# Moving the gates, the carry factor and the squares of a state-space kernel between engines, with a new order per stage

## The chip, the cores and the metric

The kernel runs on one core of a Trainium2 chip. The metric is the device time of one execution in microseconds (us), the median of several runs. Everything is float32.

## What is computed

Input x has 8 sequences of 1024 steps and 256 channels. The first half is a selective state-space layer (512 inner channels, 16 states each), the second a mixture of 8 experts, top 2, with capacity 768; both have a residual and a layer norm. The part that matters here:

```python
xn = x * rsqrt(mean(x * x) + 1e-6) * norm_w
x_branch, gate = split(xn @ W_in.T)
xc = causal_conv4(x_branch) + conv_b
xc = xc * sigmoid(xc)
dt = soft_clamp(softplus(xc @ W_dt.T + b_dt), 0.001, 0.1, 0.5)      # a tanh
Bp, Cp = xc @ W_B.T, xc @ W_C.T
dA = exp(soft_clamp(dt[..., None] * A, -8, 8, 0.5))                 # tanh, then exp
# for each step t:
h = h * dA_t + dt_t * B_t * x_t                                     # h: 8 x 512 x 16
if t % 10 == 0: h = h * min(20 / (norm(h) + 1e-8), 1)               # one norm per sequence
y_t = h . C_t + D * x_t
out = x + scale * (y * gate * sigmoid(gate)) @ W_out.T
```

## The kernel before

`ssm_phase` walks 52 stages of 20 time steps for all 8 sequences. A stage is cut into four quarters q (10 steps for 4 sequences), a quarter into four sequences u; `s` = 0 to 15 numbers these slots. Each engine has its own program, one loop over i (stage) and s (slot) with `if s == ... and ok(i + k)` blocks, and runs it strictly in that order; semaphores `s_...` tie the programs together. So the place of a block in an engine's list decides what waits behind it. Work for stage i+2 or i+3 is prepared while stage i is scanned.

- **VectorE** has per slot `mult` (L579, dt x B, 640 elements) and `scan` (L610, 704 elements, the recurrence over 10 steps); every two slots `carry` (L596) puts the start state, already multiplied by the norm factor (CAR), into PSUM. It adds `norm_sum` (L617), `z_out` (L631), `dt_x` (L566), the gate products XC (L647, slot 6) and SG (L705, slot 15), VV (L697), and the copy of the router logits LGS (L714).
- **ScalarE** computes the decays in DA: 64 tangents per stage (L514, spread over the slots by the list `DUE`) and four large exponentials (`exp_a`, L377). It also makes the squares SQ for the norm (L398) and of x (L408), copies out of PSUM (L417, L423, L458 to L467, L475), the tangents of the two gates, since x sigmoid(x) = x/2 (1 + tanh(x/2)) (L430, L499), and the dt chain of exponentials, logarithm and tangent (L451, L481, L489). Two activation tables are loaded per stage, at L481 and L489.
- **GpSimd** multiplies H by C (L775), makes the norm factor FC by a power of -0.5 (L755) and CAR (L760), and does DT (L737), XN (L743), the layer norm of VV, and DX.
- **TensorE** sums H C over the 16 states by identity matmuls (`y_sum`, L820; each fp32 matmul shows as two records, 34 records per quarter with L816), the norms (L862), the sum of squares of x (L873), the projections of branches and gates (`project`, L826), the convolution as diagonal matmuls (L836) with its bias (L832), dt (L845), B and C (L902), the output projection (L921), transposes (L911), and router logits (L930). All but the y sums share two PSUM banks, PA and PZ, in turn; `wait_free` waits for the reader of the use before.

The order of the shared banks before, and where a stage's gate is released:

```python
        users_pa = [
            (3, s_ms, lambda j: j + 1),
            (2, s_xb, lambda j: j + 1),
            (2, s_xc, lambda j: j + 1),
            (2, s_ex, lambda j: 4 * j + 2),
            (-2, s_x2t, lambda j: j + 1),
            (1, s_sg, lambda j: j + 1),
            (-2, s_lgs, lambda j: j + 1),
        ]
```

`moe_phase` with the experts follows and is not touched.

## Time and profile before

| | |
|---|---|
| median of 3 runs | 2773.73 us (2773.64 to 2775.39) |
| span of the profiled execution, first to last instruction | 2772.7 us |
| PE, DVE, ACT, POOL busy | 94%, 86%, 81%, 77% of the span |
| mean granted TensorE clock | 0.975 of full speed |
| scan phase | to about 2315 us of the span |

PE is TensorE, DVE VectorE, ACT ScalarE, POOL GpSimd. The profiled execution has no time of its own besides its span; the runs' median is 1.0 us above it. A duration in the timeline holds the end of an instruction, during which the next already runs, so the step from start to start is shorter than the duration. The granted clock is a share of full speed: 1.00 is 2.4 GHz, 0.50 is 1.2 GHz.

### The profile page before, as it was taken

To read this page: it belongs to the slowest core of one execution; us is meant where nothing else is said; L and a number is where in the kernel's file an instruction comes from. 1 tells how busy PE (TensorE), PEld (TensorE's weight loads), DVE (VectorE), ACT (ScalarE), POOL (GpSimd) and SP (SyncE) were. 2 spreads that over 40 slices of the span, in tenths; PEclk is the share of its full clock that TensorE was granted. 3 is DMA by queue.
4 is the path that set the end of the run, shared out by engine and by line. 5 is a ranking of instruction groups with operands and counts; after the bars stand their busy time and mean duration, and the time that the engine had idled before them with its cause. 6 is when DMAs were issued, how large, how long until landed. Compare 5 with 4: busy or idle time off the path is not lost. (4 is left out here: it accounts for less than half of the span.)

```text
span 2772.7 us, 50775 instructions
## 1 busy us (share of the span) xinstructions
PE 2593.0 (94%) x16812; PEld 2388.8 (86%) x16812; DVE 2382.4 (86%) x3391; ACT 2245.1 (81%) x5074; POOL 2134.4 (77%) x2237
## 2 busy tenths in 40 slices
PE   5899999999999999999999999999999986899992
PEld 4899999999999999999999999999999975677762
DVE  2999999999999999999999999999999997221124
ACT  5999999999999999999999999999999962111113
POOL 0789888898898988989889889898898883434314
PEclk9899999999999999999999999999999987999996
DMA  1222222222222222222222222222222222234227
GB/s 61 70 78 78 79 80 78 78 78 81 77 78 75 80 79 78 78 78 82 78 78 78 81 78 78 76 78 80 78 78 78 75 78 93 48 93 105 61 48 254
DMA packets 145746, 225.65 MB, mean 81 GB/s; under 512 B 37836, under 2 KB 84684, under 8 KB 144332
## 3 DMA queue, kind: packets, MB, share of 16 engines
q1 hardware_dynamic: 123044, 188.95, 22.4%
q0 software_dynamic: 9216, 12.59, 2.6%
q10 hardware_dynamic: 13224, 20.86, 2.2%
q8 instruction: 134, 2.20, 0.3%
q14 instruction: 128, 1.05, 0.1%
HBM read 189.27 MB, written 33.05 MB: 80 GB/s over the span
## 5 line engine op out<-in xcount | busy, mean ns | idle before, releaser
L775 POOL TENSOR_TENSOR H<-H,CB 128x640 f32<-128x640 f32 (+1 forms) x832 | 1216.2, 1476 | 157.1 <-DVE H L610 154.9
L610 DVE TENSOR_TENSOR_SCAN H<-DA,PM 128x704 f32<-128x704 f32 (+1 forms) x832 | 1309.4, 1594 | 0.0
L514 ACT ACTIVATE DA<-DT,SM 128x160 f32<-128x160 f32 (+1 forms) x3328 | 1106.8, 421 | 1.6 <-POOL DT L737 0.3
L820 PE MATMUL YB<-H,ID 128*128 128x160 f32 (+1 forms) x6656 | 1043.9, 309 | 0.2 <-POOL H L775 0.2
L820 PEld LDWEIGHTS YB<-H,ID 128*128 128x128 f32 x6656 | 982.3, 191 | 16.4 <-issue 11.2
L579 DVE TENSOR_TENSOR PM<-PM,BB 128x640 f32<-128x640 f32 (+1 forms) x832 | 673.1, 809 | 0.0
L377 ACT ACTIVATE DA<-DA 128x2560 f32<-128x2560 f32 (+1 forms) x206 | 477.7, 2319 | 1.7
L755 POOL TENSOR_TENSOR FC<-SN,HALF 128x4 f32<-128x4 f32 x206 | 232.8, 1130 | 40.8 <-DVE SN L617 36.8
L826 PE MATMUL PAZ<-XN,RB 128*128 128x160 f32 x1664 | 254.7, 307 | 0.1
L836 PEld LDWEIGHTS PAZ<-XB,CD 128*128 128x128 f32 x1664 | 237.5, 188 | 16.8
L845 PE MATMUL PAZ<-XC,RB 128*128 128x160 f32 x1664 | 244.4, 300 | 3.3 <-DVE XC L647 3.3
L1285 POOL DMA_INDIRECT YA<-YS,IG x48 | 75.1, 1566 | 219.8 <-ACT YS L1116 208.2
L836 PE MATMUL PAZ<-XB,CD 128*128 128x160 f32 x1664 | 243.1, 297 | 0.0
L826 PEld LDWEIGHTS PAZ<-XN,RB 128*128 128x128 f32 x1664 | 237.9, 195 | 0.7 <-ACT CS L467 0.3
L845 PEld LDWEIGHTS PAZ<-XC,RB 128*128 128x128 f32 x1664 | 231.1, 190 | 6.4 <-DVE XC L647 4.0
L921 PE MATMUL PAZ<-WO,Z 128*80 128x256 f32 x832 | 189.1, 380 | 0.0
L862 PE MATMUL YB<-SQ,MEAN 128*128 128x128 f32 x824 | 131.3, 282 | 43.0 <-ACT SQ L398 43.0
L760 POOL TENSOR_TENSOR CAR<-H,FC 128x256 f32<-128x256 f32 x206 | 155.4, 754 | 17.3
L921 PEld LDWEIGHTS PAZ<-WO,Z 128*80 128x80 f32 x832 | 125.3, 151 | 49.4 <-issue 0.7
L1359 PE MATMUL PE<-W,HT 128*128 128x256 f32 x768 | 167.2, 379 | 0.8 <-issue 0.8
L1348 PE MATMUL PE<-XTE,W 128*128 128x384 f32 x512 | 167.3, 488 | 0.0
L1359 PEld LDWEIGHTS PE<-W,HT 128*128 128x128 f32 x768 | 145.3, 190 | 20.8 <-issue 1.3
(157 smaller groups left out, 2779.7 us busy)
## 6 DMA issues: line engine op xcount, KB each, us to landing
BB<-Bd SPq DMA_DIRECT2D x208, 320.0 KB, 3.4
CB<-Cd SPq DMA_DIRECT2D x208, 320.0 KB, 3.2
W<-in_w ACTq DMA_DIRECT2D x16, 1024.0 KB, 7.9
XT<-in_xT SPq DMA_DIRECT2D x52, 160.0 KB, 2.2
XR<-in_xp SPq DMA_DIRECT2D x208, 40.0 KB
X2d<-VV SPq DMA_DIRECT2D x208, 40.0 KB
YA<-VV SPq DMA_DIRECT2D x208, 40.0 KB
HI<-YA SPq DMA_DIRECT2D x6, 1024.0 KB, 9.9
```

The source lines that it names most:

```text
L377: eng.activation(v, v, ACT.Exp, scale=16.0).then_inc(s_da, 1)
L514: eng.activation(DA[:, c0 + k0:c0 + k1, :, a, m, 1:11].rearrange("p c b t -> p b c t"), DT[:, j % 2, a].rearrange("p b (c t) -> p b c t", ...
L579: eng.tensor_tensor(DBX(u)[:, 0:64 * k].rearrange("p (a n t) -> p a n t", a=4, n=16)[:, :, :, 1:k], U(c)[:, :, 4 * g + u, 0:k - 1].unsquee ...
L610: eng.tensor_tensor_scan(H[:, q % 3, u, 0:n], decays(c, g)[:, u], DBX(u)[:, 0:n], 0.0, ALU.mult, ALU.add).then_inc(s_scan, 1)
L755: eng.tensor_tensor(FC[:, p % 2], SN[:, p % 2], HALF[:], ALU.pow).then_inc(s_pow, 1)
L775: eng.tensor_tensor(h, h, cb, ALU.mult).then_inc(s_hc, 1)
L820: mm = eng.matmul(yv, ID[:], hv[:, :, :, n, 0:w], start=False, stop=n == 15)
L826: mm = eng.matmul(p[:, 160 * a:160 * a + 160], WIN[:, k, c0 + 128 * a:c0 + 128 * a + 128], XN[:, j % 2, k], start=k == 0, stop=k == 1)
L836: mm = eng.matmul(p[:, 160 * a:160 * a + 160].rearrange("p (b t) -> p b t", b=8), CD[:, k, 2 * m + a], XB[:, 2 * m + a, :, k:k + 20], star ...
L845: mm = eng.matmul(p[:, 160 * a:160 * a + 160], WDT[:, k, c:c + 128], XC[:, j % 2, k].rearrange("p b t -> p (b t)"), start=k == 0, stop=k == 3)
L921: mm = eng.matmul(PZ[0:80, 256 * g:256 * g + 256], zf[:, a, 80 * g:80 * g + 80], WO[:, a, :], start=a == 0, stop=a == 3)
L1359: t = eng.matmul(bank(n)[:, 256 * h:256 * h + 256], HT[:, m, 128 * (2 * c + h):128 * (2 * c + h) + 128], W2[:, e % 2, m, :], start=m == 0, ...
```

## The change

Both gates are computed by ScalarE's Silu: XC by four instructions of 160 elements, with the convolution's bias as a per-partition operand (the bias matmuls, L832, go), and SG by one of 640 elements; VectorE's L647 and L705 go. ScalarE's functions are grouped by table: a Silu set (with Tanh) from slot 0, a logarithm and exponential set from slot 11. All 64 tangents stand in slots 0 to 10, all four large exponentials in 12 to 15, and the dt chain is split, with its tangent in slot 0 of the next stage. CAR goes: the carry is multiplied by FC as a per-partition scalar, one instruction per slot; the factor 20 is folded into the matrix NORM. The squares for the norm move from ScalarE to GpSimd (slot 3 of each quarter), ahead of the last multiply by C. TensorE's blocks get other slots, and `wait_free` is replaced by explicit waits. The load of XR on SyncE moves from slot 14 to slot 2 of the next stage. The core of the diff:

```diff
+        def pa_after_gate(eng, i):
+
+            if ok(i):
+                eng.wait_ge(s_sg, i + 1)
+            if ok(i - 3):
+                eng.wait_ge(s_lgs, i - 2)
+
+        def pa_after_steps(eng, i):
+
+            if ok(i + 3):
+                eng.wait_ge(s_root, i + 4)
+            elif ok(i + 2):
+                eng.wait_ge(s_ex, 4 * (i + 2) + 2)
+            else:
+                pa_after_gate(eng, i)
...
+        def pz_after_steps(eng, i):
+
+            if ok(i + 2):
+                eng.wait_ge(s_ex, 4 * (i + 2) + 4)
+                eng.wait_ge(s_bcs, 4 * (i + 2) + 4)
+            elif ok(i):
+                eng.wait_ge(s_sg, i + 1)
+            elif ok(i - 2):
+                eng.wait_ge(s_v, i - 1)
...
-            DUE = [0, 7, 7, 10, 12, 18, 19, 27, 35, 41, 43, 50, 56, 56, 58, 64, 64]
+            DUE = [0, 3, 9, 14, 21, 27, 33, 37, 45, 51, 57, 64]
...
-                    q = 4 * i + s // 4
-                    if s % 4 == 0 and 1 <= q <= NQ - 2:
-
-                        eng.wait_ge(s_scan, 4 * q)
-                        if q >= 2:
-                            eng.wait_ge(s_nrm, q - 1)
-                        eng.activation(SQ[:], H[:, (q - 1) % 3].rearrange(
-                            "p u (a t) -> p u a t", t=11)[:, :, :, 10], ACT.Square).then_inc(s_hsq, 1)
+                    if s == 0 and (ok(i) or ok(i + 1) or ok(i + 2)):
+                        eng.preload_act_table_set(SILU)
+                    if s == 0 and ok(i + 1):
+
+                        j = i + 1
+                        eng.wait_ge(s_ln, j + 1)
+                        eng.activation(TA[:], TA[:], ACT.Tanh, bias=CST[:, 2:3], scale=KD).then_inc(s_dth, 1)
                     if s == 0 and ok(i + 3):
 
                         j = i + 3
                         eng.wait_ge(s_xt[j % 2], one(j))
-                        if ok(i):
-                            eng.wait_ge(s_sg, i + 1)
-                        elif ok(i + 1):
-                            eng.wait_ge(s_xc, i + 2)
-                        eng.activation(TB[:, 0:2].rearrange("p a b t -> p a (b t)"), XT[:, j % 2],
-                                       ACT.Square).then_inc(s_sq, 1)
-                    if s == 1 and ok(i + 3):
-                        j = i + 3
-                        eng.wait_ge(s_ssum, j + 1)
-                        if ok(i + 2):
-                            eng.wait_ge(s_br, 2 * j - 1)
                         if j > 0:
-                            eng.wait_ge(s_xn, j)
-                        eng.activation(RST[:], PA[:, 320:480], ACT.Copy).then_inc(s_ms, 1)
-                    if s == 1 and ok(i + 2):
+                            eng.wait_ge(s_ssum, j)
+                        eng.activation(SX[:], XT[:, j % 2], ACT.Square).then_inc(s_sq, 1)
...
-                    if s == 9 and ok(i + 2):
+                        if j >= 2:
+                            eng.wait_ge(s_u, 2 * j - 1)
+                            eng.wait_ge(s_dx, j - 1)
+                            eng.wait_ge(s_dtp, 2 * (j - 1))
+                        for n, (p, m) in enumerate(((PZ, 1), (PA, 0))):
+                            eng.wait_ge(s_cv, 2 * j + n + 1)
+                            for a in range(2):
+                                eng.activation(XC[:, j % 2, 2 * m + a].rearrange("p b t -> p (b t)"),
+                                               p[:, 160 * a:160 * a + 160], ACT.Silu,
+                                               bias=PV[:, 0, 2 * m + a:2 * m + a + 1]).then_inc(s_xc, 1)
+                    if s == 10 and ok(i + 2):
+
                         j = i + 2
-                        if j > 0:
-                            eng.wait_ge(s_dt, j)
-                        for n, (p, m) in enumerate(((PA, 1), (PZ, 0))):
-                            eng.wait_ge(s_dtp, 2 * j + n + 1)
-                            for a in range(2):
-                                eng.activation(TA[:, 2 * m + a].rearrange("p b t -> p (b t)"),
-                                               p[:, 160 * a:160 * a + 160], ACT.Exp,
-                                               bias=PV[:, 1, 2 * m + a:2 * m + a + 1]).then_inc(s_ex, 1)
+                        eng.wait_ge(s_dtp, 2 * j + 2)
...
+                    if s == 0 and ok(i):
+
+                        j = i
+                        eng.wait_ge(s_gt, 2 * (j + 1))
+                        if j >= 2:
+                            eng.wait_ge(s_z, 4 * (j - 1))
+                            eng.wait_ge(s_sgh, j - 1)
+                        if ok(i - 3):
+                            eng.wait_ge(s_lgs, i - 2)
+                        eng.activation(SG[:, j % 2, :, :, 1:21].rearrange("p (m a) b t -> p m (a b) t", m=2),
+                                       BOTH.rearrange("p m (n t) -> p m n t", t=20), ACT.Silu).then_inc(s_sg, 1)
+                    if s == 11:
+
+                        if ok(i + 1) or ok(i + 2) or ok(i + 3):
+                            eng.preload_act_table_set(LOGS)
+                        if ok(i + 2):
+                            j = i + 2
+                            if j > 0:
+                                eng.wait_ge(s_dt, j)
+                            for p, m in ((PA, 1), (PZ, 0)):
+                                for a in range(2):
+                                    eng.activation(TA[:, 2 * m + a].rearrange("p b t -> p (b t)"),
+                                                   p[:, 160 * a:160 * a + 160], ACT.Exp,
+                                                   bias=PV[:, 1, 2 * m + a:2 * m + a + 1]).then_inc(s_ex, 1)
+                        if ok(i + 3):
+                            j = i + 3
+                            eng.wait_ge(s_ssum, j + 1)
+                            if j > 0:
+                                eng.wait_ge(s_xn, j)
+                            eng.activation(RST[:], PA[:, 320:480], ACT.Ln, bias=CST[:, 0:1]).then_inc(s_root, 1)
+                    if s == 12 and ok(i + 1):
                         eng.wait_ge(s_z64, 64 * (i + 2))
-                        exp_a(i + 1, 0 if i >= 0 else 2)
+                    if s >= 12 and ok(i + 1) and (i >= 0 or s >= 14) and (i + 1 < NB - 1 or s < 14):
+                        exp_a(i + 1, s - 12)
+                    if s == 12 and ok(i - 2):
+
+                        j = i - 2
+                        eng.wait_ge(s_tr, j + 1)
+                        if j > 0:
+                            eng.wait_ge(s_lg, j)
+                        eng.activation(X2T[:].rearrange("p a b -> p (a b)"), PA[:, 0:320],
+                                       ACT.Copy).then_inc(s_x2t, 1)
+                    if s == 12 and ok(i + 3):
+                        j = i + 3
+                        eng.wait_ge(s_root, j + 1)
+                        eng.activation(RST[:], RST[:], ACT.Exp, scale=-0.5).then_inc(s_rs, 1)
+                    if s == 13 and ok(i + 2):
+                        j = i + 2
+                        eng.wait_ge(s_min, j + 1)
+                        eng.activation(TA[:], TA[:], ACT.Ln, bias=CST[:, 3:4]).then_inc(s_ln, 1)
...
                     if u == 0:
-                        eng.wait_ge(s_car, q - 1)
-                    eng.tensor_copy(o, CAR[:, u:u + 2]).then_inc(s_ca, 1)
+                        eng.wait_ge(s_fac, q - 1)
+                    eng.tensor_scalar(o, ends(q - 2)[:, u], FC[:, q % 2, u:u + 1], None, ALU.mult).then_inc(s_ca, 1)
...
                     if live and u % 2 == 0:
                         carry(q, u)
                         mult(q, u + 1)
...
-                    if s == 15 and ok(i + 1):
-                        j = i + 1
-                        eng.wait_ge(s_tg, j + 1)
-                        if j >= 2:
-                            eng.wait_ge(s_z, 4 * (j - 1))
-                        eng.scalar_tensor_tensor(
-                            SG[:, j % 2, :, :, 1:21].rearrange("p (m a) b t -> p m (a b) t", m=2),
-                            TB[:].rearrange("p (m a) b t -> p m (a b) t", m=2), 1.0,
-                            BOTH.rearrange("p m (n t) -> p m n t", t=20), ALU.add, ALU.mult).then_inc(s_sg, 1)
                     if s == 15 and ok(i - 2):
...
                     if s == 15 and ok(i - 2):
                         j = i - 2
                         eng.wait_ge(s_lg, j + 1)
+                        if ok(i + 1):
+                            eng.wait_ge(s_gt, 2 * (i + 1) + 1)
...
-                        eng.tensor_scalar(FC[:, p % 2], FC[:, p % 2], 1.25, 1.0, ALU.mult, ALU.min).then_inc(s_fac, 1)
-                        eng.wait_ge(s_fac, p + 1)
-                        eng.wait_ge(s_ca, 2 * (p + 2))
-                        eng.tensor_tensor(CAR[:], H[:, p % 3].rearrange("p u (a t) -> p u a t", t=11)[:, :, :, 10],
-                                          FC[:, p % 2].unsqueeze(2).to_broadcast([128, 4, 64]),
-                                          ALU.mult).then_inc(s_car, 1)
+                        eng.tensor_scalar(FC[:, p % 2], FC[:, p % 2], 1.0, 0.0, ALU.min, ALU.max).then_inc(s_fac, 1)
...
+                        if u == 3 and q <= NQ - 3:
+                            if q >= 1:
+                                eng.wait_ge(s_nrm, q)
+                            eng.tensor_tensor(SQ[:], ends(q), ends(q), ALU.mult).then_inc(s_hsq, 1)
...
+                    if s == 1 and ok(i + 2):
                         j = i + 2
                         eng.wait_ge(s_xn, j + 1)
                         if j == 0:
                             eng.wait_ge(s_pre, PRE_W)
-                        if not ok(i + 3):
-                            wait_free(eng, users_pa, i, BR0)
+                        pa_after_gate(eng, i)
                         project(j, 0, PA).then_inc(s_br, 1)
-                        wait_free(eng, users_pz, i, BR1)
                         project(j, 256, PZ).then_inc(s_br, 1)
-                    if s == 2 and ok(i + 2):
+                    if s == 4 and ok(i + 2):
                         j = i + 2
                         eng.wait_ge(s_xb, j + 1)
                         conv(j, 1, PZ).then_inc(s_cv, 1)
-                    if s == 3 and ok(i + 2):
+                    if s == 5 and ok(i + 2):
                         j = i + 2
-                        wait_free(eng, users_pa, i, CV0)
                         conv(j, 0, PA).then_inc(s_cv, 1)
-                    if s == 6 and ok(i + 2):
+                    if s == 8 and ok(i + 2):
                         j = i + 2
-                        eng.wait_ge(s_xc, j + 1)
+                        eng.wait_ge(s_xc, 4 * (j + 1))
                         dt_proj(j, 1, PA).then_inc(s_dtp, 1)
...
-                    if s == 7 and ok(i + 2):
+                    if s == 8 and ok(i + 3):
+                        j = i + 3
+                        eng.wait_ge(s_sq, j + 1)
+                        if not ok(i + 2) and j > 0:
+                            eng.wait_ge(s_root, j)
+                        for a in range(2):
+                            mm = eng.matmul(PA[:, 320:480], MEAN[:], SX[:, a], start=a == 0, stop=a == 1)
+                        mm.then_inc(s_ssum, 1)
...
-                    if s == 9 and ok(i - 2):
+                    if s == 12 and ok(i - 2):
                         j = i - 2
                         eng.wait_ge(s_x2, 2 * (j + 1))
-                        wait_free(eng, users_pa, i, TR)
+                        pa_after_steps(eng, i)
...
+                    if s == 14 and ok(i + 1):
                         j = i + 1
-                        if not ok(i - 2):
-                            wait_free(eng, users_pa, i, GT1)
+                        if ok(i - 2):
+                            eng.wait_ge(s_x2t, i - 1)
+                        else:
+                            pa_after_steps(eng, i)
                         project(j, 512, PA).then_inc(s_gt, 1)
-                    if s == 13 and ok(i + 1):
+                    if s == 15 and ok(i + 1):
                         j = i + 1
-                        wait_free(eng, users_pz, i, GT0)
+                        if ok(i - 1):
+                            eng.wait_ge(s_v, i)
+                        else:
```

## Rows read from the trace of the kernel before

**Rows 1.** Stretch: length, busy PE PEld DVE ACT POOL, clock, DMA share, GB/s.
```profile
500.00:1800.00 1300.00, 1277.43 (x8849) 1215.39 (x8848) 1300.00 (x1759) 1249.42 (x2781) 1151.13 (x1211) 1.00 0.27 78
...
1016.40:1059.30 42.90, 42.15 (x292) 40.09 (x292) 42.90 (x60) 41.23 (x94) 38.02 (x41) 1.00 0.26 78
```

**Rows 2.** Timeline of DVE: start us, us, engine, line, operation, tiles, count.
```profile
1032.23 0.80 DVE L647 SCALAR_TENSOR_TENSOR XC<-TB,PAZ 128x640 f32<-128x640 f32 x1
1032.95 0.28 DVE L596 COPY PM<-CAR 128x128 f32<-128x128 f32 x1
1033.15 0.82 DVE L579 TENSOR_TENSOR PM<-PM,BB 128x640 f32<-128x640 f32 x1
```

**Rows 3.** Timeline of PE in the same stage, idle time before in brackets.
```profile
1017.07 0.71 PE L862 MATMUL YB<-SQ,MEAN 128*128 128x128 f32 x4 [0.73 <-ACT SQ L398]
1017.61 0.71 PE L873 MATMUL PAZ<-TB,MEAN 128*128 128x160 f32 x4
1018.16 2.34 PE L826 MATMUL PAZ<-XN,RB 128*128 128x160 f32 x16
...
1022.37 0.70 PE L832 MATMUL PAZ<-SM,ID 128*128 128x320 f32 x2
1022.92 2.34 PE L836 MATMUL PAZ<-XB,CD 128*128 128x160 f32 x16
...
1040.29 1.69 PE L820 MATMUL YB<-H,ID 128*128 128x160 f32 x10
```

**Rows 4.** Timeline of ACT over the same 43 us.
```profile
1005.24 1.28 ACT L481 ACT_TABLE_LOAD   x1
1006.54 0.83 ACT L481 ACTIVATE TA<-TA,CST 128x640 f32<-128x640 f32 x1
...
1011.47 0.70 ACT L499 ACTIVATE TB<-PAZ 128x640 f32<-128x640 f32 x1 [0.78 <-PE PAZ L826]
...
1030.25 2.33 ACT L377 ACTIVATE DA<-DA 128x2560 f32<-128x2560 f32 x1
1032.48 5.54 ACT L514 ACTIVATE DA<-DT,SM 128x160 f32<-128x160 f32 x17
1037.91 0.64 ACT L398 ACTIVATE SQ<-H 128x256 f32<-128x256 f32 x1
...
1040.37 1.21 ACT L451 ACTIVATE TA<-PAZ,SM 128x160 f32<-128x160 f32 x4
...
1042.21 2.98 ACT L514 ACTIVATE DA<-DT,SM 128x160 f32<-128x160 f32 x9
```

**Rows 5.** POOL's groups in that stage: count | busy us, mean ns | idle before.
```profile
L775 POOL TENSOR_TENSOR H<-H,CB 128x640 f32<-128x640 f32 x17 | 25.0, 1484 | 2.9 <-DVE H L610 2.9
...
L760 POOL TENSOR_TENSOR CAR<-H,FC 128x256 f32<-128x256 f32 x4 | 3.0, 754 | 0.3
...
L737 POOL TENSOR_SCALAR DT<-TA 128x640 f32<-128x640 f32 x1 | 0.7, 724 | 0.1
```

**Rows 6.** Granted clock (third from the end) in two microseconds near the end.
```profile
2221.00:2223.00 2.00, 1.92 (x7) 1.96 (x8) 2.00 (x3) 2.00 (x5) 1.99 (x3) 0.50 0.14 40
```

**Rows 7.** Timeline of PE around its longer idle pieces.
```profile
115.10 1.22 PE L862 MATMUL YB<-SQ,MEAN 128*128 128x128 f32 x4 [3.16 <-ACT SQ L398]
...
2221.08 0.87 PE L816 MATMUL YB<-DX,ID 128*128 128x160 f32 x2 [2.37 <-DVE Z L631]
2221.74 7.22 PE L820 MATMUL YB<-H,ID 128*128 128x160 f32 x32
...
2231.26 0.52 PE L816 MATMUL YB<-DX,ID 128*128 128x160 f32 x2 [1.85 <-DVE Z L631]
2231.62 4.78 PE L820 MATMUL YB<-H,ID 128*128 128x160 f32 x32
...
2273.89 0.52 PE L816 MATMUL YB<-DX,ID 128*128 128x160 f32 x2 [2.00 <-DVE Z L631]
2274.25 6.39 PE L820 MATMUL YB<-H,ID 128*128 128x160 f32 x32
```

192 lines of the change are left out of this document (54 added, 138 removed).

## The prediction

> **What bounds the kernel now.** I read five views, in this order. The shares of busy time by stretch come first: from 500 to 1800 us VectorE is busy for all of the 1300 us, TensorE for 1277, ScalarE for 1249, GpSimd for 1151, at a granted clock of 1.00, and one loop stage lasts 42.90 us (from one first multiply of a stage to that of the next) [rows 1]. So VectorE sets the pace, but the reader is to see that TensorE and ScalarE are within 2% and 4% of it: a change that only shortens VectorE's list can win no more than they allow, and one that makes two of these engines wait for each other in turn can lose. The timeline of VectorE then gives the step from one instruction to the next (instructions run a little into each other, so a step is less than a duration) [rows 2]; those of TensorE, ScalarE and GpSimd give the same for theirs [rows 3 to 5]. In steady state TensorE idles once per stage, 0.73 us ahead of the norm matmuls [rows 3]. Last come the granted clock and the idle pieces of TensorE at the start and end of the phase, where it idles longer [rows 6, 7].
>
> **The change part by part, VectorE.** Two instructions of 640 elements go, L647 and L705; L647 takes 0.72 us from start to start [rows 2], L705 has its shape, so 1.44 us per stage. Eight carry copies of 128 elements at 0.20 us [rows 2] become sixteen multiplies of 64 elements by a partition's scalar. The trace has no such instruction. Bounds: half a copy (0.10 us, nothing lost) and a whole copy (0.20 us, 1.6 us lost per stage). I take the line through the 640-element step, 0.72 us, and the 128-element step, 0.20 us, which gives 0.07 us + 1.02 ns per element, 0.135 us for 64 elements; 16 x 0.135 - 8 x 0.20 = +0.56 us. VectorE's list becomes 42.90 - 1.44 + 0.56 = 42.0 us, between 41.5 and 43.1.
>
> **GpSimd.** The four carry multiplies of 256 elements (0.75 us each) go, four squares of the same shape come, which I price the same [rows 5]. Bounds for a square: from half (one operand, read twice) to twice that, -1.5 to +3 us on a list of 38.0 us [rows 1]; nothing of it reaches the end, since GpSimd keeps at least 2 us per stage.
>
> **TensorE.** The bias matmuls, two records of 0.55 us together, go twice per stage (1022.37 to 1022.92) [rows 3]. Its list becomes 42.90 - 0.73 idle - 1.10 = 41.07 us.
>
> **ScalarE's list** loses four squares (0.64 us less the 0.11 by which an instruction runs into the next, seen from 17 tangents that show 5.54 us and yield after 5.43 [rows 4]) and a copy, and gets three more small instructions for the convolution's gate: about 2 us less. By lists alone all four engines would be at or under 42.0 us.
>
> **The order, which is what I take to decide.** In the new code the matrix work hangs on ScalarE's place in a closed ring, once round per stage, with both engines in program order:
> 1. TensorE at step 1 projects the branches of stage i+2 only after ScalarE's Silu of gate i (pa_after_gate waits for s_sg of i+1). In the old code this release was a VectorE instruction at the end of the stage before.
> 2. TensorE works without a wait up to the projections of dt and B, C at step 9. ScalarE waits for them at step 10, ahead of its copies of B and C.
> 3. ScalarE then has everything in one run: 7 tangents, the load of the logarithm set, 4 exponentials, a logarithm, the copy of x2, a small exponential, four large exponentials, another logarithm, the load of the Silu set, the tangent of dt. GpSimd turns that into DT, ScalarE waits for DT, does 3 tangents, and only then Silu of the gate, which lets TensorE go on.
>
> TensorE's half. From the branches' start to the end of B and C, 1018.16 to 1040.29, the old order takes 22.13 us [rows 3]. Out of it go 1.10 us of bias; into it come the sum of squares of x (1017.61 to 1018.16, 0.55), one more norm pair (1017.07 to 1017.61, 0.54), and ten more records of the y sum (32 take 4.78 us [rows 7], so 1.49). 22.13 - 1.10 + 0.55 + 0.54 + 1.49 = 23.61 us, 23.7 with a handover.
>
> ScalarE's half [rows 4, 5]: four exponentials and four copies 1.84 (1040.37 to 1042.21); 7 tangents at 5.43/17 = 0.319, 2.24; two loads at 1.30 (1005.24 to 1006.54) and 0.1 each for the instruction ahead of a load that can't run into it, 2.80; two small ones of 160 elements priced as tangents, 0.64; four large exponentials at 2.23 (1030.25 to 1032.48), 8.92; copy of x2, just over a tangent's step, 0.33; logarithm of 640 elements 0.83 - 0.11 = 0.72; tangent of dt 0.83, since the next waits for its end; DT on GpSimd 0.72 with 0.15 for two handovers; 3 tangents 0.96; Silu at the price of the tangent of the same 640 elements from PSUM, 0.70, with 0.05. Sum 20.90 us. The square of x hides behind DT. GpSimd is free for DT by then: after the last scan it has XN, a square, and one multiply left, some 3 us (the last two 0.75 and 1.48 [rows 5]), and the scans end more than 5 us before.
>
> The ring is 23.7 + 20.9 = **44.6 us**, 1.7 over today's stage and 2.6 over VectorE's new list. Unknown prices on it: Silu of 640 elements, which no row shows. Bounds are nothing and twice its neighbour, 43.9 to 45.3 us. The other four new Silus lie in the half where ScalarE waits for TensorE anyway; there ScalarE has 54 tangents (17.2 us), the copy of the branches (0.6) and these four (1.2, as the four exponentials) against 23.7 us, so over 3 us cover them, and without the cover they would cost their 1.2. So VectorE's saving goes nowhere: it waits about 2.6 us a stage, late at the copy of the logits (step 15), which now waits for the gate projection (s_gt).
>
> The loads are the one term where a page says more than the rows. Here a load shows 1.28 us and the next activation starts 1.30 us after it began [rows 4]. The Trainium skill, page ScalarE: Activation LUTs, section What ACT_TABLE_LOAD costs, gives about 1283 ns for the load and about 1380 ns of drain with it. The load agrees; the drain doesn't appear beside these loads. By the page the ring would be an estimated 2.8 us longer, 47.4 us; by the rows it is 44.6.
>
> **What TensorE's idle time does.** Its list is 41.07 us, so it idles 3.5 us per round. About 0.5 lies ahead of the transposes, which wait for the logarithm of step 11 (29.6 us into the round, TensorE gets there at 23.6 + 5.0 + 0.5); the other **3.0 us are one piece**, right ahead of the branches. The trace shows what such pieces do. After 3.16 us TensorE's records double (1.22 us against 0.71 for four); after 2.37 us the clock is granted at 0.50, the 1.2 GHz level; after 2.00 us the 32 records of the y sum take 6.39 us in place of 4.78. After 1.85 us, and after every 0.73 us of the steady state, it stays at 1.00, 2.4 GHz [rows 1, 3, 6, 7]. One fall costs, over a y sum of 34 records: after 2.37 us 0.66 + 7.22 = 7.88 against 0.36 + 4.78 = 5.14, +2.7 us; after 2.00 us 0.36 + 6.39 = 6.75, +1.6 us [rows 7]. I take the middle, 2.2 us. This work is the first of TensorE's half of the ring, so it is paid in full, and as the list grows with the ring the idle piece stays 3.0 us and the fall comes again in the next stage. With a fall in nine stages of ten the stage is 44.6 + 2.0 = **46.6 us**.
>
> The ring runs for stages 0 to 49 (both i and i+2 exist), 50 times. 50 x (46.6 - 42.9) = +185 us. The start (branches of stage 2 after the gate of stage 0) comes out within some 3 us of today's by the same sum with short tangents; in stages 50 and 51 VectorE saves 2 us and may wait some for the last tangents; the expert part is untouched. I add nothing for them, +-5 us. The profiled execution spans 2772.7 us, 1.0 us under the runs' median of 2773.7, and 1 us lies around it, so 2773.7 + 185 = 2959, **2960 us**. Its own range: 1.6 to 2.7 us per fall, in 8 to 10 of 10 stages, gives 45.9 to 47.3 us, 2923 to 2995.
>
> **Rivals.**
> A. *The ring holds but the clock does not fall* (or seldom). For it: 1.85 us of idling left it alone, and some of the 3.0 us may be broken up by a late record. Against: each piece of 2.00 us and over that I found was followed by slow records. 44.6 us: 2773.7 + 50 x 1.7 = 2859 us. Chance 0.17. In between, a fall in every second stage: 2870 to 2920, chance 0.10.
> B. *VectorE goes on setting the pace*, the other side. It needs the ring below 42.9 us, 1.7 less than the sum. VectorE's list of 42.0 over 52 stages then gives 2773.7 - 52 x 0.9 = 2727 us. For it: every list is shorter, and VectorE has no idle time to lose today. Against: no single term of ScalarE's half but the tangents, the large exponentials and the two loads is as large as 1.7 us, and all those have rows. Chance 0.07. Between the two, a result within 0.2% of 2774 (5.5 us, about what a measurement of this kernel tells from no change) has 0.03.
> C. *Something else is late on top*: GpSimd's squares at twice the price, DT waiting behind a multiply (1.48 us [rows 5]), VectorE's norm sums waiting for norm matmuls that come later. It would add 1 to 2 us to the round, 3005 to 3060 us. Chance 0.02.
> D. *Each load drains ScalarE on the ring.* If a load held the engine by as much again as it lasts, two of them would add 2.6 us: 47.2 us without falls, 2989 us, and over 3050 with them. The rows have no such gap. Chance 0.01. The Trainium skill's sentence on the drain, named above, is what speaks for it.
>
> **How the numbers follow.** My forecast, ring and falls, has 0.60, its rivals 0.17, 0.10, 0.07, 0.03, 0.02 and 0.01. The time is the likeliest's, 2960. The range takes in A and the middle: 2845 to 3000, with 0.87 less what spills over its ends. Faster 0.07, same 0.03, slower 0.90.
>
> **What would show it.** VectorE no longer at 1300 of 1300 but near 90%, its idle time ahead of the logits' copy. ScalarE idle some 3 us (more with falls) ahead of the copy to BS, released by the B, C matmuls. TensorE idle about 3.0 us ahead of the branch projection, released by ScalarE's Silu into SG. The granted clock of 500 to 1800 us under 1.00, some 0.95 if it falls each stage for 3 to 6 us. GpSimd idle ahead of DT, released by the tangent. I would be wrong if VectorE stays without idle time, if ScalarE reaches step 10 after TensorE has B and C, or if the clock row stays at 1.00 with the wait there.

## The result and the profile after

The changed kernel takes 3074.4 us (median of four runs, 3073.0 to 3075.5), the kernel before 2774.6 beside it: a ratio of 1.108, 95% interval 1.1065 to 1.1096, 300 us slower. The prediction said 2960 with a range of 2845 to 3000. The sign and the kind of cause were right, but the time lies outside the range, and 115 us were missing. The profiled execution spans 3071.0 us. With 50 stages in the phase that is (3071.0 - 2772.7)/50 = 6.0 us more a stage: 48.9 us instead of 42.9. Below, stages are worked out this way from each run's time, or from the starts of one line far apart.

Busy time by stretch, and the granted clock (third from the end) as the branches start, to be held against [rows 1, 6]:

```profile
500.00:1800.00 1300.00, 1169.53 (x7657) 1102.80 (x7658) 1167.46 (x1703) 1045.79 (x2404) 999.42 (x1067) 0.95 0.24 69
...
1042.00:1044.00 2.00, 2.00 (x9) 2.00 (x9) 2.00 (x6) 0.57 (x2) 1.37 (x2) 0.50 0.13 36
```

No engine is at its limit now: TensorE and VectorE are busy for 90% of the stretch, ScalarE for 80%, GpSimd for 77%, and each waits for another. One round in the timelines. First TensorE, against [rows 3]:

```profile
1023.61 0.47 PE L886 MATMUL PAZ<-ID,VV 80*128 80x80 f32 x4 [0.60 <-ACT RST L499]
1023.92 3.62 PE L896 MATMUL PAZ<-WO,Z 128*80 128x256 f32 x16
...
1040.75 4.05 PE L806 MATMUL PAZ<-XN,RB 128*128 128x160 f32 x16 [3.26 <-issue]
```

ScalarE, against [rows 4]:

```profile
1017.51 0.29 ACT L434 ACTIVATE BS<-PAZ 16x160 f32<-16x160 f32 x1 [3.11 <-PE PAZ L877]
...
1023.05 0.41 ACT L499 ACTIVATE RST<-PAZ,CST 128x160 f32<-128x160 f32 x1
...
1033.66 1.28 ACT L393 ACT_TABLE_LOAD   x1
1034.96 0.83 ACT L398 ACTIVATE TA<-TA,CST 128x640 f32<-128x640 f32 x1
...
1039.00 1.10 ACT L466 ACTIVATE DA<-DT,SM 128x160 f32<-128x160 f32 x3 [2.85 <-POOL DT L716]
1039.97 0.68 ACT L479 ACTIVATE SG<-PAZ 128x640 f32<-128x640 f32 x1
```

So the predicted ring is there, with its wait of ScalarE ahead of BS, its 0.6 us ahead of the transposes, and TensorE's idle piece of 3.26 us ahead of the branches (the gate's Silu ends at 1039.97 + 0.68 = 1040.65, they start at 1040.75), after which 16 records take 4.05 us instead of 2.34 and the clock is granted at 0.50 (1.2 GHz). From BS to the end of the tangent is 18.3 us, as summed. What the prediction did not have lies in the 2.85 us that ScalarE then waits for DT. VectorE, against [rows 2], and GpSimd, against [rows 5]:

```profile
1015.01 0.32 DVE L591 TENSOR_SCALAR PM<-H,FC 128x64 f32<-128x64 f32 x1
1015.24 0.82 DVE L576 TENSOR_TENSOR PM<-PM,BB 128x640 f32<-128x640 f32 x1
...
1027.63 0.32 DVE L626 TENSOR_TENSOR Z<-YB,SG 128x160 f32<-128x160 f32 x1 [4.66 <-issue]
...
1033.62 1.61 DVE L605 TENSOR_TENSOR_SCAN H<-DA,PM 128x704 f32<-128x704 f32 x1
```

```profile
1035.25 0.87 POOL L722 TENSOR_TENSOR XN<-XT,RST 128x320 f32<-128x320 f32 x1 [0.57 <-PE PAZ L806]
1036.08 0.65 POOL L754 TENSOR_TENSOR SQ<-H 128x256 f32<-128x256 f32 x1
1036.68 1.47 POOL L755 TENSOR_TENSOR H<-H,CB 128x640 f32<-128x640 f32 x1
1038.23 0.73 POOL L716 TENSOR_SCALAR DT<-TA 128x640 f32<-128x640 f32 x1
```

VectorE stands 4.66 us ahead of z_out, and that is its only wait from 500 to 1800 us (us in total, times, longest):

```profile
DVE Z L626 <- issue: 132.5, 26, 6.1
```

"Issue" says that the profile names no releaser, but the code does: z_out of a stage's first quarter waits for s_op, since Z is one buffer and the output projection of the stage before still reads it. The projection ends at 1027.54 (1023.92 + 3.62), z_out starts at 1027.63. It used to be in slot 10 and is now in slot 12, behind a wait for ScalarE's logarithm (RST). So VectorE's last scan of the stage ends at 1035.23, only 0.6 us ahead of the end of the tangent (1034.96 + 0.83 = 1035.79), and GpSimd has XN, which also waited for the gate matmuls, a square and a multiply (1035.25 to 1038.15) ahead of DT.

The prediction's sum then closes with two numbers corrected. ScalarE's half, BS 1017.51 to branches 1040.75, is 23.24 us (predicted 20.9, and 2.3 of DT); TensorE's half is the rest of 48.9, 25.7 us (predicted 23.7 + 2.0 for the clock; e9 below tells the two apart).

### The profile page after: what moved, and what is told of

Same layout as the page of the kernel before. It is cut to its first block and busy times, and to the rows that moved or that the text cites. A ratio compares the mean times of both kernels' runs of the same rounds, so it can differ in the third digit from the quotient of the medians.

```text
span 3071.0 us, 50564 instructions
## 1 busy us (share of the span) xinstructions
PE 2681.5 (87%) x16604; PEld 2453.5 (80%) x16604; DVE 2429.3 (79%) x3702; ACT 2155.2 (70%) x4975; POOL 2108.2 (69%) x2237
## 3 DMA queue, kind: packets, MB, share of 16 engines
q8 instruction: 132, 2.16, 0.3%
## 5 line engine op out<-in xcount | busy, mean ns | idle before, releaser
L466 ACT ACTIVATE DA<-DT,SM 128x160 f32<-128x160 f32 (+1 forms) x3328 | 1084.6, 428 | 142.7 <-POOL DT L716 141.5
L800 PE MATMUL YB<-H,ID 128*128 128x160 f32 (+1 forms) x6656 | 1026.9, 310 | 0.0
L800 PEld LDWEIGHTS YB<-H,ID 128*128 128x128 f32 x6656 | 994.1, 194 | 0.0
L806 PE MATMUL PAZ<-XN,RB 128*128 128x160 f32 x1664 | 359.5, 381 | 189.5 <-issue 153.3
L806 PEld LDWEIGHTS PAZ<-XN,RB 128*128 128x128 f32 x1664 | 320.2, 251 | 210.7 <-issue 180.7
L626 DVE TENSOR_TENSOR Z<-YB,SG 128x160 f32<-128x160 f32 x208 | 62.9, 302 | 262.0 <-issue 256.5
L591 DVE TENSOR_SCALAR PM<-H,FC 128x64 f32<-128x64 f32 x824 | 265.7, 322 | 3.1 <-POOL FC L738 3.0
L814 PE MATMUL PAZ<-XB,CD 128*128 128x160 f32 x1664 | 235.3, 298 | 2.5 <-ACT XB L411 2.5
L814 PEld LDWEIGHTS PAZ<-XB,CD 128*128 128x128 f32 x1664 | 228.0, 188 | 3.3 <-ACT XB L411 3.3
```

The source lines that it names most:

```text
L466: eng.activation(DA[:, c0 + k0:c0 + k1, :, a, m, 1:11].rearrange("p c b t -> p b c t"), DT[:, j % 2, a].rearrange("p b (c t) -> p b c t", ...
L800: mm = eng.matmul(yv, ID[:], hv[:, :, :, n, 0:w], start=False, stop=n == 15)
L806: mm = eng.matmul(p[:, 160 * a:160 * a + 160], WIN[:, k, c0 + 128 * a:c0 + 128 * a + 128], XN[:, j % 2, k], start=k == 0, stop=k == 1)
L814: mm = eng.matmul(p[:, 160 * a:160 * a + 160].rearrange("p (b t) -> p b t", b=8), CD[:, k, 2 * m + a], XB[:, 2 * m + a, :, k:k + 20], star ...
```

## The experiments on the ring

Eighteen kernels ran, each timed beside the kernel before (2774 to 2776). The first four each take hold of one link of the changed kernel.

**e1.** The gate's Silu goes first in its slot, so it no longer waits for DT.

> The changed kernel with one block moved on ScalarE: in slot 0 the Silu of the gate stands ahead of the square of x and of the three decay tangents that wait for DT. No list gets shorter. Ring theory: TensorE's branches then follow its norm matmuls at once (they end at 1037.4 in the profile of the changed kernel, the branches start at 1040.75), the idle piece of 3.3 us and the fall of the clock go, granted clock 1.00 in steady state; what is left is VectorE's list of 43.7 us a stage: 2774 + 50 x 1 = 2825 us (2800 to 2870). Rival, the lists are what is longer (carries on VectorE) and the order costs little: over 3030 us.

```
 s == 0:  preload SILU, Tanh of TA
+         Silu of the gate -> SG        # from behind the first tangents
          Square of x
          wait s_dt, first tangents
-         Silu of the gate -> SG
```

3014.1 us, ratio 1.086 (1.084 to 1.088), 190 us above what was expected. The idle piece and the clock's fall are gone (clock 1.00), yet a stage is 47.8 us. The waits moved. Of TensorE, VectorE and ScalarE in one round:

```profile
1026.12 0.71 PE L840 MATMUL YB<-SQ,NORM 128*128 128x128 f32 x4 [2.46 <-POOL SQ L754]
...
1036.98 0.71 PE L840 MATMUL YB<-SQ,NORM 128*128 128x128 f32 x4 [0.90 <-POOL SQ L754]
```

```profile
1053.96 0.33 DVE L626 TENSOR_TENSOR Z<-YB,SG 128x160 f32<-128x160 f32 x1 [3.97 <-issue]
```

```profile
1043.86 0.29 ACT L445 ACTIVATE BS<-PAZ 16x160 f32<-16x160 f32 x1 [4.30 <-PE PAZ L877]
```

There is a second ring, that is, a second closed chain of waits: output projection, z_out, VectorE's scans, the square on GpSimd, norm matmuls, then dt and B, C on TensorE, BS, the logarithm on ScalarE, transposes, output projection. It closes at 47.8 us, in every stage alike, and never touches the branches.

**e3** makes seven tangents earlier (off the run of step 3), **e4** fills TensorE's idle piece with twelve matmuls whose result nobody reads, for which the gate's Silu waits.

> The changed kernel with the list DUE as [0, 3, 9, 14, 21, 28, 35, 41, 49, 56, 64, 64]: seven decay tangents are done before ScalarE waits for the B, C matmuls and not after. They fit into its wait of 3.1 us. If the ring runs only through ScalarE's list from there to the gate's Silu, the stage gets 2.2 us shorter: 2962 us. If it runs through the transposes, the output projection and z_out on VectorE, TensorE gets there only 0.7 us earlier, since it still has its y sum ahead of them: 3074 - 50 x 0.7 = 3037 us. If no ring holds, 3074 us.

```
-DUE = [0, 3, 9, 14, 21, 27, 33, 37, 45, 51, 57, 64]
+DUE = [0, 3, 9, 14, 21, 28, 35, 41, 49, 56, 64, 64]
```

> The changed kernel with 12 matmuls of 128 x 128 x 128 put ahead of TensorE's wait for the gate's Silu; they fill 2.7 of the 3.3 us of idling with work that nobody reads (into free columns of PZ, and the Silu waits for them, which they should have ended before). If the idle piece makes the clock fall and the fall is paid on the ring: granted clock 1.00, branches in 2.3 us and not 4.1, 1.8 us less per stage, 3074 - 90 = 2984 us. If the slow matmuls are hidden: 3074 us. If the filling delays the ring: over 3074 us.

```
 s == 1:
+    12 x matmul(PZ[:, 320:448], MEAN, ID)   -> s_fill
     wait s_sg, s_lgs
     project(branches)
 ScalarE, Silu of the gate:
+    wait s_fill
```

3015.8 and 3015.9 us (both 1.088, 1.086 to 1.089), neither of them a time that was expected. Two of the three runs, e1 and e4, are on the same floor: 47.8 us in every stage from BS to BS, without a fall of the clock. That is the second ring, and what these two gained, some 59 us, is all that lay between the two rings. e4 removed the falls and little else, and gained 58 us where they were priced at 2.0 us a stage (100): then the floor holds. e3 ends at the same time by chance. Its stages differ, 47.1 us without a fall and 47.7 or 48.8 with one, so it is not on that floor: ScalarE's half became 0.8 us shorter (22.45 from 23.24), and the clock fell a little less often.

**e2, e9.** Z in two buffers opens the second ring; e2 also makes XN after DT.

> The changed kernel with the two waits removed that hold back DT on GpSimd and that the prediction did not have: Z has two buffers, so that z_out of a stage's first quarter does not wait for the output projection of the stage before, and XN is made after DT in slot 0, not ahead of the last square in slot 15. (The norm uses the matrix MEAN and the factor 1.25 as in the kernel before, to make room.) Theory that these two are the whole of what the prediction missed: DT is ready 2.3 us earlier, ScalarE waits under 1 us for it, stage 46.5 us, 3074 - 50 x 2.3 = 2960 us, as predicted. Rival, another path through TensorE or GpSimd stands right behind: 3030 to 3070 us. Rival, the fall of the clock is what was mis-sized: no change at all, 3074 us.

> The changed kernel with Z in two buffers and nothing else (room for it: the norm's matmuls use the MEAN matrix and the factor is scaled by 1.25 before the minimum). Ring theory: the ring of the changed kernel goes through the output projection, the wait of z_out for it, VectorE's last quarter, and XN, square, multiply and DT on GpSimd, to the tangents; with Z twice, z_out's 4.7 us wait goes, and what is left is the ring through the branches with XN still ahead of DT. XN waits for TensorE's gate matmuls. If XN is what remains late, this stays near the run with XN moved as well (2915) or above it, up to 2990; if XN never mattered, it gives 2915 or less. Rival (the wait of z_out is only a symptom of a late stage): no change from 3074.

```
-Z = sb("Z", [128, 4, 8, 20])
+Z = sb("Z", [128, 2, 4, 8, 20])       # NORM's room; MEAN and a factor 1.25
 z_out, first quarter:
-    wait s_op >= j
+    wait s_op >= j - 1
 GpSimd (e2 alone):
-    s == 15: XN   (ahead of the last square and multiply)
+    s == 0:  DT, then XN
```

e9: 2976.6 (1.073, 1.071 to 1.075), the wait of z_out gone; e2: 2915.3 (1.050, 1.048 to 1.052). Both edits count, 98 and 61 us. ScalarE's half of the ring goes from 23.24 to 21.91 us in e9 and 20.87 in e2 (BS at 1014.64 to branches at 1035.51), the predicted 20.9 to the digit. So Z was worth 1.3 us a stage and XN 1.0, together the 2.3 us that the prediction lacked, and its sum for this half was right for a GpSimd that is on time.

But e2 was expected at 2960 and is 45 us below. The clock is why. In e9 the idle piece ahead of the branches is 3.26 us in each stage, as in the changed kernel, and in 9 of 45 stages in steady state the clock does not fall behind it. Two stages, one after the other:

```profile
961.79 2.41 PE L805 MATMUL PAZ<-XN,RB 128*128 128x160 f32 x16 [3.26 <-issue]
...
1007.32 4.09 PE L805 MATMUL PAZ<-XN,RB 128*128 128x160 f32 x16 [3.26 <-issue]
```

The first round takes 45.53 us (961.79 to 1007.32), the next 47.18 (to 1054.50). TensorE's half, branches to BS, is 23.6 us without a fall, 25.3 with a short fall and about 26.1 with one that lasts longer. So in one and the same kernel a fall costs 1.7 us, or 2.5. The changed kernel has one in every stage, and its 25.7 us is 23.6 and 2.1 for the falls, against 23.7 and 2.0 predicted. In e2 the idle piece is 2.72 us, and behind it the clock falls in 21 of 45 stages only:

```profile
1035.51 2.41 PE L805 MATMUL PAZ<-XN,RB 128*128 128x160 f32 x16 [2.72 <-POOL XN L721]
```

Its stages are 45.1 us without a fall and 46.1 or 47.4 with one, 45.7 in the mean; of the 24.3 us of TensorE's half without a fall, 0.4 is a wait for GpSimd's squares.

## The experiments on VectorE's list

**e7, e8.** The new carry alone, in the kernel before, where VectorE paces and every step counts whole. e8 multiplies by the constant 1.0 instead of the partition's factor, so the norm's factor is left out of its result.

> The kernel before with the carry part of the change alone: sixteen multiplies of 64 elements by a partition's scalar, CAR gone. VectorE has no idle time there, so each 0.1 us in its list shows. With the step of 0.235 us that the changed kernel's timeline shows: 16 x 0.235 - 8 x 0.20 = 2.2 us a stage, 2774 + 52 x 2.2 = 2886 us. With the prediction's price of 0.135 us: 2803 us. If the step is stretched by something in the changed kernel alone, nearer to 2803.

> As e7, but each carry multiplies by the constant 1.0 and not by the factor in FC (the norm factor is left out of the recurrence; all else runs as before). If reading the scalar from memory per partition is what takes 0.1 us: step 0.135 us, 2803 us. If it is the small strided instruction itself: 2886 us as e7.

```
-    tensor_copy(o, CAR[:, u:u + 2])                          # 128 elements, 8 a stage
+    tensor_scalar(o, ends(q - 2)[:, u], FC[:, q % 2, u:u + 1])  # 64, 16 a stage
```

2884.0 us (1.039, 1.038 to 1.041) and 2835.8 (1.022, 1.020 to 1.024). In the timeline of e7 the carry steps 0.24 us, in that of e8 0.18:

```profile
1003.27 0.35 DVE L594 TENSOR_SCALAR PM<-H,FC 128x64 f32<-128x64 f32 x1
1003.51 0.84 DVE L579 TENSOR_TENSOR PM<-PM,BB 128x640 f32<-128x640 f32 x1
```

```profile
1023.78 0.25 DVE L594 TENSOR_SCALAR PM<-H 128x64 f32<-128x64 f32 x1
1023.96 0.81 DVE L579 TENSOR_TENSOR PM<-PM,BB 128x640 f32<-128x640 f32 x1
```

The scalar read from a partition costs 48 us over some 820 carries, 0.06 us each. The rest of the way to the predicted 0.135 us, which would have given 2803, is where the values come from: the copies read CAR, where they lie side by side, the multiplies every eleventh element of H. In e11 below copies of 128 elements read H:

```profile
1010.28 0.37 DVE L592 COPY PM<-H 128x128 f32<-128x128 f32 x1
1010.56 0.82 DVE L575 TENSOR_TENSOR PM<-PM,BB 128x640 f32<-128x640 f32 x1
```

They step 0.29 us in the mean, those from CAR 0.19. Half of that 0.10 for half the elements, added to 0.135, gives an estimate of 0.185, near the 0.18 of e8.

**e10.** The carries of the changed kernel brought back to eight copies, the factor multiplied by GpSimd in place.

> The changed kernel with its carries brought back to eight copies of 128 elements (0.20 us each by their step in the kernel before), the factor multiplied on GpSimd in place into the ends of H (0.75 us a quarter). VectorE's list is 2.2 us a stage shorter. Ring theory: only what VectorE does between z_out and the last scan lies on the ring, one to two quarters of carries, 0.5 to 1.0 us a stage, less what GpSimd's multiply of 0.75 us adds to the ring ahead of DT: 3015 to 3075, no more. List theory (VectorE paces, so its price counts whole): 2965.

```
 GpSimd, u == 2:
+    tensor_tensor(ends(p), ends(p), FC broadcast)  -> s_car
 VectorE:
-    16 x tensor_scalar(o, ends(q - 2)[:, u], FC[..])
+    8 x tensor_copy(o, ends(q - 2)[:, u:u + 2])
```

3054.4 us (1.101, 1.099 to 1.103), 20 us less than the changed kernel. Where a ring paces, a 2 us shorter list is worth the part of it that lies on the ring, and no more.

**e5, e6, e11** put the edits together: e5 Silu first and Z twice; e6 also the seven tangents and the carries as eight multiplies of 128 elements by a broadcast factor; e11 as e6 with the carries of e10.

> The changed kernel with the Silu of the gate ahead of the wait for DT and with two buffers for Z; XN stays in slot 15. The first cuts the ring through DT, the second the ring that e1, e3 and e4 all stopped at (47.8 us a stage: output projection, z_out, three quarters of scans, norm matmuls, B and C, ScalarE, transposes, output projection). Two-ring theory: neither is left, VectorE's own list of 43.7 us sets the pace, 2774 + 50 x 0.9 = 2820 us (2800 to 2850), granted clock 1.00, VectorE without idle time. Rival, a third ring over 45 us: 2880 us or more. If the effects only add (60 us of e1 and about 40 for Z), 2975 us.

> As e5, with the seven tangents early (e3) and with the carry as one tensor-by-tensor multiply for two sequences (eight per stage, 128 elements, factor broadcast) in place of sixteen multiplies by a partition's scalar. Theory: no ring, VectorE's list 42.9 - 1.4 = 41.5 us, TensorE's 41.1 and up to 0.6 of waits: 41.7 to 42.2 us a stage, 2774 - 50 x 0.9 = 2729 us (2715 to 2760), faster than the kernel before. Rival: the new multiply reads two SBUF operands and collides with GpSimd's multiplies; each would then take up to 0.5 us and not 0.2, 2.4 us more a stage, 2850 us.

> The changed kernel with the gate's Silu first in its slot, Z in two buffers, seven tangents early, and the carries as eight copies with the factor multiplied in place by GpSimd. VectorE's list: 42.9 less 1.44, 41.5 us, plus at most 1.3 for dt_x beside GpSimd; TensorE's 41.1; GpSimd's 38.0 busy plus four squares of 0.65, 40.6, with its waits on VectorE near its list's end. Expected 2740 (stage 42.2), between 2705 and 2790. Rival (the collision of VectorE with GpSimd's multiplies is general and not only for instructions with two SBUF inputs): above 2850.

```
 e6, VectorE:
-    16 x tensor_scalar(o, ends(q - 2)[:, u], FC[..])
+    8 x tensor_tensor(o, ends(q - 2)[:, u:u + 2], FC[:, q % 2, u:u + 2] broadcast)
```

2889.9 (1.042, 1.040 to 1.044), 3011.1 (1.085, 1.083 to 1.087) and 2890.3 us (1.042, 1.040 to 1.044): three misses by 70 to 280 us. The second ring went all the same: e5 is e1 with Z in two buffers, and 124 us below it. Their timelines show one thing that the kernel before never does. e6's carry on VectorE:

```profile
1009.19 0.37 DVE L591 TENSOR_TENSOR PM<-H,FC 128x128 f32<-128x128 f32 x1
...
1026.45 2.30 DVE L591 TENSOR_TENSOR PM<-H,FC 128x128 f32<-128x128 f32 x1
```

e11's dt_x on VectorE, and GpSimd beside the second of them:

```profile
1016.63 0.48 DVE L562 TENSOR_TENSOR PM<-DT,XC 128x320 f32<-128x320 f32 x1
1027.15 2.88 DVE L562 TENSOR_TENSOR PM<-DT,XC 128x320 f32<-128x320 f32 x1
```

```profile
1026.78 2.90 POOL L757 TENSOR_TENSOR H<-H,CB 128x640 f32<-128x640 f32 x2
1029.64 1.25 POOL L735 TENSOR_TENSOR FC<-SN,HALF 128x4 f32<-128x4 f32 x1
```

The same instruction takes 0.48 or 2.88 us; the long one ends 0.35 us after GpSimd's pair of multiplies. Both inputs are in SBUF, in dt_x as in e6's carry; the multiplies by BB and the scans have one input in PSUM and never stretch (0.80 to 0.83 and 1.58 to 1.62 us in e11). The Trainium skill, SBUF — State Buffer, section Who interferes with whom, states this: a VectorE instruction with two SBUF inputs contends with a GpSimd instruction that reads SBUF, and the order of issue decides which of the two is blocked. By that rule the trace agrees, and goes further in one point: the 2.88 us lasted through two multiplies in a row. e6 and e11 differ only in the carry, the factor applied by VectorE with two inputs in SBUF or by GpSimd ahead of a copy, and lie 121 us apart.

**e13** puts the collision alone into the kernel before, by moving dt_x.

> The kernel before with one edit: each stage's two dt_x multiplies (both inputs in SBUF, 0.49 us each there) stand one scan later on VectorE, behind the second scan of their pair. By the trace of before they then start some 3 us later, at about 1026.3 and 1037.2, while GpSimd runs a pair of H multiplies (1025.65 to 1028.57 and 1036.60 to 1039.5) and not, as now, its short chain of factors. Collision theory (a VectorE multiply with two SBUF inputs stands until GpSimd's running multiplies end): each takes 2 to 3 us, 4 to 5 us more a stage on the engine that paces: 2975, between 2875 and 3030. Rival (ports are independent, and the long dt_x in the changed kernels has another cause, such as a wait for its data): within 0.3% of before.

```
-    s == 2, s == 6:  dt_x, then scan
+    s == 3, s == 7:  scan, then dt_x
```

2834.6 us (1.022, 1.020 to 1.024), below the expected range, but not the rival's: the mean of dt_x went from 493 to 1110 ns, and 2 x 0.617 x 50 = 62 us is the 60 measured. It slipped in between the two multiplies of a pair here, so it waited for one.

## The experiments that close the account

**e12, e14, e15.** To e11: squares on ScalarE again (e12); then CAR as a buffer again, with XN behind (e14) or ahead of (e15) GpSimd's last multiply.

> As the run before it, with the four squares of H's ends on ScalarE as in the kernel before (0.4 us each there), 2.6 us a stage less on GpSimd. If GpSimd's list or its squares ahead of the norm's matmuls hold the stage there, this is 20 to 60 us faster than that run; if VectorE paces both, the same within 0.3%; if ScalarE's waits in its own order for the scans hold back the Silu's chain, slower by 20 or more.

> The fourfold edit with the squares on ScalarE, and three more things: CAR as a buffer of its own again (the copies then read contiguous values, 0.20 us a step instead of 0.28), the squares of x written into TA so that there is room for it, and XN behind the last multiply of the stage on GpSimd, where its wait for the gate matmuls (3.2 us a stage in the last run) no longer makes GpSimd late for the first quarter. VectorE's list: 42.9 less 1.44, 41.5, if dt_x falls back to 0.5 us. Collision theory: GpSimd on time means that dt_x falls into its short factor chain again, mean under 700 ns, stage 41.5 to 42.8: 2740, between 2705 and 2780, that is faster than or equal to before. Rival (the ring still holds, or TensorE waits for XN now): above 2790.

> As the run before it, but XN stays ahead of the last multiply, as in the changed kernel. Collision theory: GpSimd is held 3.2 us by TensorE's gate matmuls, is late for the first quarter, and the first dt_x of the stage still takes about 1.6 us; VectorE's list is 41.5 plus 1.1 to 1.4: stage 42.6 to 43.5, 2760 to 2810, slower than the run before it by 20 to 60 us. Rival: the same as that run, within 0.3%, if XN's place never mattered.

```
 e12, ScalarE, s % 4 == 0:
+    wait s_scan;  activation(SQ, ends(q - 1), Square)
 GpSimd, u == 3:
-    tensor_tensor(SQ, ends(q), ends(q))
 e14 and e15:
-SX = sb("SX", [128, 2, 160])   # x squared goes to TA[:, 0:2], at s == 2
+CAR = sb("CAR", [128, 4, 64])
 e14, GpSimd:
-    s == 15: XN, last multiply
+    s == 15: last multiply;  s == 0: XN, DT
```

2853.1 (1.028, 1.027 to 1.030), 2807.1 (1.012, 1.010 to 1.014) and 2869.7 us (1.035, 1.033 to 1.037). XN's place is worth 63 us, more than expected. Both are above their ranges, and neither reached the kernel before. From e12 to e15 XN stands still, and CAR and the squares of x in TA cost 17 us together; so XN's place is all that e14 gained over e12. I still held VectorE to pace them, short of its 1.5 us a stage at the logits' copy.

**e16, e17.** e16 moves the logits' copy behind the next stage's first multiplies, e17 also the second dt_x from slot 6 to slot 10.

> The version with XN behind the last multiply, and VectorE's copy of the logits (which waits for a gate matmul, so as not to read a bank that TensorE writes) moved from the end of a stage behind the first two multiplies and the carry of the next, 2.3 us later. There VectorE stood 44.6 us in 1300 (1.5 a stage) for it; its list without that is 42.1. List theory: all of it comes back, stage 42.1 to 42.5, 2735, between 2725 and 2765: faster than the kernel before. Rival (the wait moves on: VectorE then waits in the same place for the gate's Silu or the logits' copy holds the branches): 2780 to 2810.

> The run before it with the stage's second dt_x multiply moved from slot 6 to slot 10 on VectorE. In that run it took 2.43 to 2.50 us in slot 6 (the first one, in slot 2, 0.48), since GpSimd came late out of its DX and H multiplies; behind the sum of slot 10 GpSimd was on time in the version before (its factor chain waited 0.34 us for that sum). Collision theory: both then take 0.5 us, VectorE's list falls by 2.0 to some 41.6, close to TensorE's 41.1: stage 41.6 to 42.4, 2730, between 2710 and 2755, faster than the kernel before. Rival (VectorE, now early again, runs into the next multiply of GpSimd, or into TensorE's list, and the time stays): 2790 to 2810, with the dt_x mean above 1200 ns or a wait in its place.

```
 VectorE:
-    s == 15: LGS <- PA        (waits for the gate matmuls)
+    s == 0 of the next stage, ahead of the scan: LGS <- PA
 e17:
-    s == 6:  dt_x(2i + 2)
+    s == 10: dt_x(2i + 2)
```

2807.7 and 2806.9 us (both 1.011, 1.0095 to 1.013): nothing. In e16 the wait went and dt_x grew by just as much. Groups of e14, then of e16:

```profile
L579 DVE TENSOR_TENSOR PM<-DT,XC 128x320 f32<-128x320 f32 x60 | 43.8, 729 | 0.3 <-issue 0.3
L711 DVE COPY LGS<-PAZ 80x16 f32<-80x16 f32 x30 | 5.1, 171 | 44.6 <-issue 44.6
```

```profile
L579 DVE TENSOR_TENSOR PM<-DT,XC 128x320 f32<-128x320 f32 x60 | 88.0, 1466 | 0.3 <-issue 0.3
```

VectorE is busy 1298 of 1300 us in e16 and still does not set the time: a collision is booked as busy time, so an engine that is early looks full. My theory of e5 to e16, that VectorE's list paces, falls with it. What the three versions have in common is TensorE. Its waits, e17 from 500 to 1800 us:

```profile
PE YB L856 <- ACT SQ L397: 38.8, 60, 0.9
PE YB L856 <- ACT SQ L421: 21.5, 30, 0.7
```

That is 2.0 us a stage for the squares of H's ends, and with 41.5 us of work 43.5, the stage of all three. The same sum fits e12 (86.4 us of such waits, 2.9 a stage: 44.4) and e15 (96.9 us, 3.3: 44.8). An engine's work and waits always add up to the stage; what the sums say is that TensorE waits for nothing but the squares, and whether that sets the time needs a run. **e18** moves the norm matmuls of slots 4 and 8 behind the projections of their slots.

> The run before it with TensorE's norm matmuls of slots 4 and 8 moved behind the convolution half and the dt half of the same slot (2.3 us each). Three versions with different waits and lengths on VectorE all took 43.5 us a stage; in all three TensorE waits 0.72, 0.41 and 0.88 us a stage (60.3 us in 1300) for ScalarE's squares and does 41.5 us of work: together 43.5. TensorE theory: the waits of slots 4 and 8, 1.29 us, are filled with the projections, stage 42.2: 2742, between 2725 and 2775, faster than the kernel before. Rival (the sums of the norms then come late to VectorE, whose slack there is 2.4 to 2.7 us, and the squares to ScalarE; the stage stays): 2790 to 2815.

```
 TensorE:
     s == 4:  y_sum(q - 2, 11, 16)
-             norm matmuls
              conv half (s == 8: dt half)
+             norm matmuls
```

2712.5 us, ratio 0.9775 (0.976 to 0.979): 94 us less than e17, 62 less than the kernel before, and 30 more gained than I had put down, below the expected range. Its waits of TensorE, and its busy time by stretch:

```profile
PE YB L824 <- ACT SQ L421: 22.1, 31, 0.7
```

```profile
500.00:1800.00 1300.00, 1277.87 (x8979) 1226.08 (x8979) 1300.00 (x1745) 1281.07 (x2937) 1182.73 (x1248) 1.00 0.29 81
```

VectorE is at 1300 of 1300 with dt_x at 641 ns, so this time I take it to pace: 42.9 - 1.44 for the two removed instructions, and 2 x 0.15 for dt_x, gives 41.8; measured 42.9 - 62.5/50 = 41.65.

## Why the prediction was right or wrong

- **VectorE loses 1.44 us** (L647, L705): right, as far as e18 shows, where the time comes out by VectorE's list again (41.8 expected from it, 41.65 measured).
- **Carries +0.56 us**: mis-sized. A step is 0.235 us (1015.01 to 1015.24), so 16 x 0.235 - 8 x 0.20 = +2.16, above the upper bound of 0.20 a piece. The line through the two sizes left out that the scalar is read from a partition and the values from every eleventh element. e7 shows 109 us for it. VectorE's list was 43.6, not 42.0. On the ring it counted for little (e10: 20 us).
- **TensorE's half 23.7, ScalarE's half 20.9**: right, 23.6 in e9's stages without a fall, and 20.87 in e2.
- **The step that failed** is "GpSimd is free for DT by then ... the scans end more than 5 us before". I priced GpSimd's work behind the scans but took the scans' end from the old order. They end 0.6 us before the tangent does. OP went from slot 10 to 12 with Z in one buffer, and the wait of z_out for it holds VectorE 4.66 us; XN waits for the gate matmuls and stands ahead of a square, a multiply and DT. The diff shows both moves, and I followed neither past its engine. The two cost 2.3 us a stage, 115 us, just what the forecast lacks, and e2 takes both away. Two of the signs named were off for the same reason: GpSimd did not idle ahead of DT, and VectorE, busy for 90% as forecast, idled at z_out and not at the logits.
- **A rival was missing**: the second ring through OP at 47.8 us, which e1 and e4 hit. Rival C had the kind of thing ("something else is late on top") at 1 to 2 us and 0.02; its 3005 to 3060 came nearest.
- **The clock**: right that it falls in nearly each stage (0.95 over 1300 us; 4.05 for 2.34 us), and right in size: 2.1 us a stage by e9's stages with and without a fall, against 2.0. The reading behind it, slow records after each idle piece of 2.00 us and over, was too sharp. In the kernel before, a piece of 2.67 us was followed by four records at full speed, while one of 1.90 us was followed by slow ones. Full speed also followed 24 of 45 pieces of 2.72 us in e2, and 9 of 45 of 3.26 us in e9. That the clock fell behind all 45 in the changed kernel was partly luck.

```profile
2239.06 0.71 PE L862 MATMUL YB<-SQ,MEAN 128*128 128x128 f32 x4 [2.67 <-ACT SQ L398]
...
2241.95 0.87 PE L816 MATMUL YB<-DX,ID 128*128 128x160 f32 x2 [1.90 <-DVE Z L631]
```

- **Rival D, a drain with each load**: not seen. The tangent starts 1.30 us after the load did (1033.66, 1034.96), with a load of 1.28.
- **Squares on GpSimd** at the price of the carry multiplies: 0.65 us against 0.75, right in size. But "nothing of it reaches the end" was wrong: in the changed kernel 0.6 us of it stands in the chain ahead of DT (1036.08 to 1036.68), and where the rings are open e12 gains 37 us over e11 by taking them off GpSimd, with the lateness they bring to TensorE and to dt_x.

What stays open: why the clock falls behind one idle piece and not behind another of the same length; how the 17 us from e12 to e15 divide between CAR and the squares of x in TA; and what set the time of e6 and e11.

## What to carry to other kernels

When a change moves a producer to a later slot, list every single buffer that it reads or writes and go on to who waits there, on the other engines too, until the chain comes back to where it began; where such a ring is longer than every engine's list, it is the stage. After taking one ring away, expect the next, and look for it by what several edits have in common; but compare them stage by stage, since equal times can be chance (e3). An engine at 100% busy is not proven to pace: look whether its instructions have grown.
